# Attention scores: 64 keys for early queries, key halves added in PSUM, two banks in turn

## The reference

```python
xn = layernorm(x, g_in)
q = (xn @ Wq) * 64 ** -0.5            # 16 heads
k, v = split(xn @ Wkv)                # one head of keys and values, shared by all 16
k, v = concat(null_k, k), concat(null_v, v)
sim = q @ k.T + bias                  # bias per head; causal mask and key mask
attn = softmax(sim)
out = layernorm((attn @ v) @ Wo, g_out)
return x + out
```

## Time and profile before

| | |
|---|---|
| time of the kernel, median of 3 runs (lowest to highest) | 1219.02 us (1218.99 to 1219.39) |
| profiled execution, span from first to last instruction | 1217.0 us |
| instructions in it | 34049 |
| DVE busy | 980.3 us, 81% |
| ACT busy | 984.2 us, 81% |
| POOL busy | 831.1 us, 68% |
| HBM traffic | 47 GB/s over the span |

### The profile page before, as it was taken

One profiled execution on the slowest core, in us unless ns is written; L12 is line 12 of the kernel. 1 busy time (PEld: TensorE's weight loads), 2 busy tenths in 40 slices (PEclk: granted clock), 3 DMA queues, 4 the chain that ended last, 5 costly groups with the idle time before them and its releaser, 6 DMA issues.

```text
span 1217.0 us, 34049 instructions
## 1 busy us (share of the span) xinstructions
PE 1181.3 (97%) x8320; PEld 1090.5 (90%) x8320; DVE 980.3 (81%) x4249; ACT 984.2 (81%) x3434; POOL 831.1 (68%) x1528
## 2 busy tenths in 40 slices
PE   4799999999999999999999999999999999999996
PEld 4699999999999999999999999999999999999994
DVE  5778888888788788887888788788887888788873
ACT  4868887888888888887888888888887888888873
POOL 3746776677677676766677677676766677677676
PEclk8889999999999999999999999999999999999998
DMA  6101111111111111111111111111111111111011
GB/s 185 69 20 55 38 48 44 36 55 54 37 45 45 37 54 55 36 50 40 36 55 54 37 48 41 37 54 55 36 53 37 36 55 54 37 51 39 18 36 53
DMA packets 39282, 58.47 MB, mean 48 GB/s; under 512 B 9792, under 2 KB 13376, under 8 KB 39104
## 3 DMA queue, kind: packets, MB, share of 16 engines
q1 hardware_dynamic: 39104, 56.91, 14.6%
HBM read 40.11 MB, written 16.78 MB: 47 GB/s over the span
## 4 chain that ended last, share of the span: by engine, by line
PE 90%; POOL 3%; issue 2%; DVE 2%; ACT 0%; POOLq 0%; DVEq 0%
PE ps_proj L461 32%; PE ps_o L454 28%; PE ps_s L416 10%; PE ps_wt L426 7%; PE ps_pv L440 7%; PE ps_pv L443 3%; PE ps_proj L478 2%; POOL bias_b L864 1%; POOL w_nrm L873 1%; PE ps_proj L488 1%; POOL y_nrm L909 0%; DVE q_sb L628 0%; DVE s_low L536 0%; POOL y_out L913 0%; POOL wo_lo L951 0%
## 5 line engine op out<-in xcount | busy, mean ns | idle before, releaser
L873 POOL TENSOR_TENSOR w_nrm<-exp_bot,w_inv 128x256 f32<-128x256 f32 x256 | 157.5, 615 | 317.6 <-DVE w_inv L557 315.1
L864 POOL TENSOR_TENSOR bias_b<-bias_c,mask_add 128x256 f32<-128x256 f32 (+1 forms) x512 | 297.6, 602 | 0.2
L461 PE MATMUL ps_proj<-xt_hi,wq_hi 128*128 128x256 f32 x1024 | 292.0, 285 | 2.1 <-DVE q_sb L628 1.8
L461 PE MATMUL ps_proj<-xt_lo,wq_hi 128*128 128x256 f32 x1024 | 291.3, 284 | 0.0
L461 PE MATMUL ps_proj<-xt_hi,wq_lo 128*128 128x256 f32 x1024 | 291.1, 284 | 0.0
L800 ACT CAST q_sb<-ps_proj 64x256 fp32r<-64x256 f32 x512 | 187.6, 366 | 111.9 <-PE ps_proj L461 96.1
L628 DVE TENSOR_TENSOR q_sb<-ps_proj,q_sb 64x256 fp32r<-64x256 f32 x512 | 216.0, 422 | 21.7 <-ACT q_sb L800 10.3
L454 PE MATMUL ps_o<-wo_hi,o_hi 128*128 128x512 f32 x512 | 223.8, 437 | 0.2 <-DVE o_lo L570 0.2
L748 ACT ACTIVATE exp_bot<-logit_bot,neg_max 128x129 f32<-128x129 f32 x512 | 202.3, 401 | 10.3 <-DVE neg_max L548 6.0
L454 PE MATMUL ps_o<-wo_lo,o_hi 128*128 128x512 f32 x512 | 203.0, 396 | 0.0
L454 PE MATMUL ps_o<-wo_hi,o_lo 128*128 128x512 f32 x512 | 202.9, 396 | 0.0
(11 more groups left out here) (92 smaller groups left out, 2573.2 us busy)
## 6 DMA issues: line engine op xcount, KB each, us to landing
x_in<-in_x_dram SPq DMA_DIRECT2D x32, 512.0 KB, 3.4
x_res<-in_x_dram SPq DMA_DIRECT2D x64, 256.0 KB, 2.7
out_dram<-y_out SPq DMA_DIRECT2D x64, 256.0 KB, 2.0
w_raw<-in_L_cond_Wq_dram SPq DMA_DIRECT2D x4, 512.0 KB, 6.0
w_raw<-in_L_cond_Wo_dram SPq DMA_DIRECT2D x4, 512.0 KB, 3.8
mask_u<-in_mask_BxS_bk_dram SPq DMA_DIRECT2D x32, 32.0 KB, 3.2
bias_c<-in_fside_16xSxS_dram SPq DMA_DIRECT2D x4, 128.0 KB, 6.7
y_nrm<-in_L_cond_Wkv_dram SPq DMA_DIRECT2D x1, 256.0 KB, 3.1
```

The lines of the kernel that those rows point to most:

```text
L461: mm = pe.matmul(ps[:, 0:TOK], w[:, k, cols], xt[:, k], start=(j == 0), stop=(j == len(todo) - 1))
L864: ins = nc.gpsimd.tensor_tensor(out_, bias, key_mask, ALU.add)
L873: ins = nc.gpsimd.tensor_tensor(out_, w_exp[:, s, :, 0:keys_], w_inv[:, s, 2 * i:2 * i + 2].unsqueeze(2).to_broadcast([P, 2, keys_]), ALU. ...
```

## The change

The score of a late query is now the sum of two matmuls of 128 columns (high keys, then low keys) added in the same place of PSUM. Early queries are scored with the first 64 high and first 64 low keys in one matmul of 128 columns. All of a step's scores fit one bank, and steps take two banks in turn. PE waits for the reads of step n-2 in place of step n-1, in one wait, and signals once. DVE adds low-key scores to the bias for the early queries only; for the late ones `logits` reads the bias itself. POOL's wait for a free `bias_b` is now on `s_read`.

```diff
-        s_low = sb("s_low", [P, BOT + TOP])
+        s_low = sb("s_low", [P, 2, HALF])
...
-        ps_s = psum("ps_s", [P, HC, 2, N])
+        ps_s = [psum(f"ps_s{i}", [P, 2, 2, N]) for i in range(2)]
...
-                for late in (1, 0):
-
-                    wait(pe, s_read, 2 * n - late)
-                    for e in range(2):
-                        mm = pe.matmul(ps_s[:, 2 * (1 - late) + e].rearrange("p a n -> p (a n)"),
-                                       q_sb[:, slot, c, e, 2 * b + late].rearrange("p u n -> p (u n)"),
-                                       keys[:, slot, b].rearrange("p a n -> p (a n)"), start=True, stop=True)
-                    mm.then_inc(s_done, 1)
+                wait(pe, s_read, 2 * (n - 1))
+                ps = ps_s[t % 2]
+                for e in range(2):
+                    early = q_sb[:, slot, c, e, 2 * b].rearrange("p u n -> p (u n)")
+                    mm = pe.matmul(ps[:, 1, e].rearrange("p (a n) -> p a n", a=2), early, keys[:, slot, b, :, 0:HALF],
+                                   start=True, stop=True)
+                for e in range(2):
+                    late = q_sb[:, slot, c, e, 2 * b + 1].rearrange("p u n -> p (u n)")
+                    for a in range(2):
+                        mm = pe.matmul(ps[:, 0, e], late, keys[:, slot, b, a], start=(a == 0), stop=(a == 1))
+                mm.then_inc(s_done, 1)
...
-                wait(dve, s_done, 2 * n + 2)
+                wait(dve, s_done, n + 1)
                 wait(dve, s_read, 2 * n)
-                for i, (out_, bias) in enumerate(zip(bot_top(s_low), bot_top(bias_b[:, s]))):
-                    nc.vector.tensor_tensor(out_, ps_s[:, 2 * i:2 * i + 2, 1, 0:out_.shape[2]], bias,
-                                            ALU.add).then_inc(s_low_made, 1)
+                low = ps_s[s][:, 1].rearrange("p e (a n) -> p e a n", a=2)[:, :, 1]
+                nc.vector.tensor_tensor(s_low[:], low, bot_top(bias_b[:, s])[1], ALU.add).then_inc(s_low_made, 1)
...
                 wait(dve, exp_made, n - 1)
-                for i, (low, out_) in enumerate(zip(bot_top(s_low), (logit_bot[:, s], logit_top[:, s]))):
-                    wait(dve, s_low_made, 2 * n + 1 + i)
-                    apart(dve)
-                    keys_ = low.shape[2]
+                apart(dve)
+                for i, (bias, out_) in enumerate(((bot_top(bias_b[:, s])[0], logit_bot[:, s]), (s_low, logit_top[:, s]))):
+                    if i == 1:
+                        wait(dve, s_low_made, n + 1)
+                        apart(dve)
+                    keys_ = (N, HALF)[i]
                     for e in range(2):
                         ins = nc.vector.tensor_tensor_reduce(
-                            out_[:, e, 0:keys_], ps_s[:, 2 * i + e, 0, 0:keys_], low[:, e], -1.0, 0.0, ALU.add, ALU.min,
+                            out_[:, e, 0:keys_], ps_s[s][:, i, e, 0:keys_], bias[:, e], -1.0, 0.0, ALU.add, ALU.min,
                             neg_max[:, s, 2 * i + e:2 * i + e + 1])
                     ins.then_inc(s_read, 1)
...
-                wait(pool, s_low_made, 2 * (n - 1))
+                wait(pool, s_read, 2 * (n - 1))
```

## The result

| | before | changed |
|---|---|---|
| time, median of 4 runs (lowest to highest) | 1219.01 us (1218.23 to 1219.39) | 1253.98 us (1253.22 to 1254.43) |
| profiled execution, span | 1217.0 us | 1252.2 us |

The change makes the kernel slower: ratio 1.0288, 95% interval 1.0276 to 1.0301, or +35 us. The forecast was 1261 us, +42.

What follows compares the result with a forecast made beforehand. PE, busy 97% of the span, was taken as the bound: +46.6 us for scores and -4.7 for the removed wait make +41.9 on a 1217.0 us span, 1258.9, plus 2.0 to the median: 1261 us, range 1185 to 1290.

Steps and rivals of the forecast that it cites:

- The bound: Whole kernel: PE, busy 97% of the span, bounds it; whatever PE is given or spared in a step moves the end.
- The price of a matmul of 128 columns: PE's scores: 0.107 us each, six 0.642 against 0.46 a step, +46.6 us over 256 steps.
- The load's own row: Loads behind the transposes: one cannot follow another in less than 0.10 us; at that price +36 us.
- Two loads of the same weights: Late queries' two halves share a stationary operand, yet each matmul has its own load: 8832 of each, 512 more.
- The rival in which the second is skipped: PE's scores: repeated weights not reloaded, block 0.543 us, +21 - 4.7, 1235 us; chance 0.05.
- columns decide: PE's scores: loads hide behind matmuls of 128 columns, time goes by columns, -29.4 - 4.7, 1185 us; chance 0.14.
- a cheaper load: PE's scores: spacing 0.073 us as for 64-column transposes, -5.6 - 4.7, 1209 us; chance 0.11.
- loads uncovered: PE's scores: short matmuls served much slower or each load exposed whole, 0.205 us a matmul, +197, 1411 us; chance 0.13.
- The wait that goes: PE's scores waiting for DVE's reads of step n-1: 36 waits at 0.13 us lost, removed by two banks, -4.7 us.
- DVE at 0: DVE's scores_low loses its 128x256 instruction, 106 us less busy time, hidden under a full PE: priced at 0.
- start and tail: Where PE isn't full, shorter DVE work and longer scores roughly cancel over some ten steps: +-2 us.
- the signs named beforehand: Changed trace: load spacing 0.10 to 0.11 (wrong under 0.09, over 0.13), 8832 loads, waits gone, chain share 13%, DVE 874 us.

Runs made afterwards that it cites:

- cols_64: Kernel before with all four scores matmuls of a step moving 64 columns in place of 256, same number of loads; 1215.42 us, ratio 0.9971.
- cols_192: Kernel before with all four scores matmuls of a step moving 192 columns in place of 256; 1216.01 us, ratio 0.9977.
- load_64: Kernel before with the four scores matmuls moving 128 columns against 64 stationary columns, so each weight load is half as wide; 1199.05 us, ratio 0.9837.
- wait_back: Changed kernel with PE waiting for the reads of step n-1 again in place of n-2; 1254.53 us, ratio 1.0290.
- both_back: Changed kernel with PE waiting for step n-1's reads again and DVE running a 128x256 instruction more in each step; 1256.37 us, ratio 1.0303.
- dve_back: Changed kernel with a 128x256 instruction on DVE in each step again, into a tile nobody reads, two banks kept; 1255.70 us, ratio 1.0299.
- dve_light: Kernel before, PE's matmuls and waits unchanged, DVE without its 128x256 addition (late queries' low-key product left out); 1209.31 us, ratio 0.9919.
- stats_early: Kernel before with only the early queries' matmuls cut to 128 columns, plus DVE's statistics of x issued one step sooner; 1212.11 us, against 1216.83 without the latter.

## Why the prediction was right, and where it was not

- **The bound.** Right: PE at 97% before and after, and every part of its step moved the end.
- **The price of a matmul of 128 columns.** Taken as 0.107 from transposes; the six take 0.62 + 0.05 = 0.67, 0.112 each. The first of the block costs less than it seems (0.06, as its load hid behind 512 columns), and the work behind the block pays for the last load. The term is +0.20 a step, 51 us, and not 46.6. The load's own row, two loads 0.10 apart, carried the mechanism (unrounded they are 0.109 apart, so the prediction's lower end of 0.10, +36 us, was the rounding of the starts), and cols_64, cols_192 and load_64 showed that it is the load: time doesn't depend on columns from 64 to 192, and falls with the width of the weights.
- **Two loads of the same weights.** Right: 8832 loads. The rival in which the second is skipped (1235) is out, and so are *columns decide* (1185), *a cheaper load* (1209: the spacing is 0.11 even with 64 columns) and *loads uncovered* (1411).
- **The pages.** Loads of 128 columns 0.11 apart agree with what the Trainium skill (TensorE: Matmul & The Clock Gate, LDWEIGHTS) gives, 107 ns. Its 81 ns for a stream at 128 columns (same page, Back-to-back issue gap) is not what this type does here.
- **The wait that goes.** The step that was mis-sized, and its cause as well. It had -4.7 us, from 36 waits at 0.13. Of the stalls that went, those at places 5 and 13 are these waits, two a turn, and 0.13 was right for them. What the prediction did not read are places 1 and 2, 0.58 us in each of the 13 turns, where PE waits for DVE ahead of other work:

```profile
PEld ps_proj L461 <- DVE xt_lo L614: 3.7, 14, 1.1
PEld ps_wt L426 <- issue: 3.2, 13, 0.4
PEld ps_proj L478 <- DVE q_sb L628: 1.7, 8, 0.3
```

The middle row names no engine, but DVE is the likely one: before the first such load of the turn, at 631.14 us, DVE's low part of the weights (L563), which these transposes need too, ended at 631.03. All in all 11.3 us of stalls went (13 x 0.58, and 14 x 0.27 at places 5 and 13), and wait_back and both_back show that the second bank had no part in it.
- **DVE at 0.** Right for the changed kernel (dve_back +1.7 us, the loop unchanged), wrong as a statement on the kernel before: there it is worth 9.8 us (dve_light). The prediction looked at a window where PE idles for 0.02 us; most of these stalls don't show as idle time of PE, because a matmul's record stretches over them (0.76 for 0.63 in the earlier trace rows). The price of 0 rested on that.
- **The sum.** +51 for the loads, -11.3 for stalls absorbed, -4.5 in start and tail (taken as within 2): +35. Forecast: +46.6 - 4.7. The loads were 5 us too cheap, and the stalls and the ends together some 11 too small; that these errors go against each other, and leave 7 us between 1261 and 1254, is luck. Of the signs named beforehand, the spacing (0.09 to 0.13), the counts and the waits were met, the chain's share is 12% for 13%, and DVE's busy time was missed (924 for 874).

## What to carry to other kernels

Price a short matmul by the load that must follow it: where each matmul has a load of its own, narrowing it below the width that covers the load (here a little under 256 columns, by 0.45 ns a column and a load of 0.11 us) saves nothing, and splitting it in two costs a load. And a stall found in the trace of before is worth its time only as long as the bound engine keeps its pace: lengthen that engine's step and stalls vanish for free, shorten it and they eat the gain. Compare equal steps of a loop with each other to find stalls that busy time and idle time hide.

## What the runs showed of the hardware

Each time the loop jumps back, 13 times in all, DVE stands still for some 2.5 us ahead of the first `s_low`, waiting for nothing that the profile shows ("issue", 33.5 us in 14 times before, 33.3 in 15 after the change). Such a turn first, then the last turn, which is written out behind the loop and needs no jump:

```profile
623.39 0.62 DVE L536 TENSOR_TENSOR s_low<-ps_s,bias_b 128x256 f32<-128x256 f32 x2 [2.50 <-issue]
```

```profile
1131.41 0.28 DVE L604 TENSOR_SCALAR mask_add<-mask_u 128x256 f32<-128x256 uint8 x1
1131.61 0.61 DVE L536 TENSOR_TENSOR s_low<-ps_s,bias_b 128x256 f32<-128x256 f32 x2
```

The stalls at places 1 and 2 go with it. In the kernel before, the last turn and the loop's first one, both entered without a jump, have no such gap, and their places 1 and 2 take 3.07 and 4.68, just as 9 and 10; in the 13 turns behind a jump they take 3.15 to 3.49 and 4.96 to 4.99. The changed kernel has the 13 gaps too, but no stall of PE behind them. What holds DVE at the jump was not tried, so that stays open; at 0.29 + 0.29 = 0.58 us of PE a turn its stalls are the largest of those found in the kernel before, and stats_early still has them.
